# A graph network on one core: the last five edge steps of a layer written out in an order of their own

## What is computed

```python
msg = jax.nn.relu(h[src] + edge_attr) + EPS_MSG
m = msg * t
seg_max = jax.ops.segment_max(m, dst, num_segments=N)
ex = jnp.exp(m - seg_max[dst])
denom = jax.ops.segment_sum(ex, dst, num_segments=N)
agg = jax.ops.segment_sum(msg * (ex / denom[dst]), dst, num_segments=N)
z = jax.nn.relu(_layernorm((h + agg) @ w1 + b1, g1, bb1))
return z @ w2 + b2
```

## Time and profile before

| what | value |
|---|---|
| median of three runs | 8966.54 us |
| the profiled execution: its time | 8967.96 us |
| the profiled execution: its span | 8966.2 us |
| VectorE busy | 6407.4 us, 71% |
| GpSimd busy | 6370.8 us, 71% |
| ScalarE busy | 3236.4 us, 36% |
| TensorE busy | 1074.9 us, 12% |
| DMA | 1288 MB, 144 GB/s on average |

### The profile page before, as it was taken

The page is one execution under the profiler, slowest core; times in us unless marked ns, Lnnn a source line. Parts: engine busy times, 40 slices in busy tenths (PEclk is TensorE's granted clock), DMA queues, the critical chain, the costliest instruction groups (busy, mean ns, idle before and its releaser), DMA issues.

```text
span 8966.2 us, 43989 instructions
## 1 busy us (share of the span) xinstructions
PE 1074.9 (12%) x3019; PEld 778.9 (9%) x3019; DVE 6407.4 (71%) x10611; ACT 3236.4 (36%) x7064; POOL 6370.8 (71%) x6739
## 2 busy tenths in 40 slices
PE   4333333332100000000210000000020000000003
PEld 3222222221100000000100000000020000000002
DVE  7777777776577777777657777777756777777775
ACT  3444444443333333333333333333333333333332
POOL 6777777776477777777557777777746777777773
PEclk6555565555555555555555555555555555555555
DMA  6666666663244444444234444444423444444442
GB/s 193 202 200 206 205 203 201 204 204 123 70 142 138 136 136 139 140 137 136 92 89 136 136 139 141 137 136 136 141 74 102 138 141 138 136 136 141 139 137 66
DMA packets 439687, 1288.07 MB, mean 144 GB/s; under 512 B 159659, under 2 KB 173652, under 8 KB 361812
## 3 DMA queue, kind: packets, MB, share of 16 engines
q1 hardware_dynamic: 221668, 1049.13, 32.2%
q0 software_dynamic: 217968, 238.47, 13.1%
HBM read 575.00 MB, written 712.10 MB: 144 GB/s over the span
## 4 chain that ended last, share of the span: by engine, by line
DVE 24%; POOL 19%; DMA 14%; issue 10%; ACT 6%; PE 3%; DVEq 0%; POOLq 0%; ACTq 0%; SPq 0%
POOL gathered L501 18%; DMA gathered<-node_table,idx_s 13%; DVE rows_out L1070 5%; DVE run L1060 3%; DVE track L1030 3%; DVE run L1056 3%; DVE psum L1018 3%; DVE psum L1048 3%; DVE psum L1043 3%; ACT track L700 2%; ACT psum L707 1%; PE psum L610 1%; PE psum L627 1%; DVE psum L1158 1%; ACT psum L721 1%
## 5 line engine op out<-in xcount | busy, mean ns | idle before, releaser
L501 POOL DMA_INDIRECT gathered<-node_table,idx_s x6464 | 6102.9, 944 | 2243.0 <-issue 1892.7
L714 ACT ACTIVATE decay<-psum 128x512 f32<-128x512 f32 x808 | 482.6, 597 | 4935.6 <-DVE psum L1043 4935.6
L1010 DVE STREAM_TRANSPOSE psum<-gathered 128x512 f32<-128x512 f32 x808 | 576.8, 714 | 2140.6 <-DMA gathered<-node_table,idx_s 2140.3
L1030 DVE TENSOR_TENSOR_SCAN track<-psum,track,edges 128x256 f32<-128x256 f32 x1616 | 1110.1, 728 | 0.0
L1056 DVE TENSOR_TENSOR_SCAN run<-decay,run,psum 128x256 f32<-128x256 f32 x1616 | 1102.1, 721 | 0.0
L1060 DVE TENSOR_TENSOR_SCAN run<-decay,run,psum 128x256 f32<-128x256 f32 x1616 | 1097.0, 720 | 0.0
L1070 DVE STREAM_TRANSPOSE rows_out<-run 128x1024 f32<-128x1024 f32 x808 | 971.3, 1202 | 0.6
L543 PE MATMUL psum<-attr_s,edgew_s 128*128 128x256 f32 x1616 | 746.0, 641 | 1242.2 <-ACT made_s L646 1225.5
L700 ACT ACTIVATE track<-psum,bias_col 128x256 f32<-128x256 f32 x1616 | 679.6, 471 | 213.5 <-DVE psum L1018 163.4
L588 PE MATMUL psum<-cst,tails 128*3 128x128 f32 x48 | 10.9, 414 | 6208.9 <-DVE tails L1109 6128.2
L543 PEld LDWEIGHTS psum<-attr_s,edgew_s 128*128 128x128 f32 x1616 | 500.8, 325 | 1485.9 <-ACT made_s L646 1355.4
(11 more groups left out here) (167 smaller groups left out, 1513.2 us busy)
## 6 DMA issues: line engine op xcount, KB each, us to landing
edge_state<-rows_out SPq DMA_DIRECT2D x404, 1024.0 KB, 10.8
edges<-edge_rows SPq DMA_DIRECT2D x406, 640.0 KB
tracks<-track SPq DMA_DIRECT2D x404, 513.0 KB
gathered<-node_table,idx_s POOLq DMA_INDIRECT x6464, 2.8
edge_rows<-made_s SPq DMA_DIRECT2D x101, 640.0 KB, 9.6
attr_s<-in_attr SPq DMA_DIRECT2D x101, 512.0 KB, 10.5
made_s<-resets SPq DMA_DIRECT2D x101, 128.0 KB
node_table<-tab SPq DMA_DIRECT2D x27, 224.0 KB, 2.4
```

The lines of the kernel that those rows point to most:

```text
L501: pool.indirect_dma_start(gathered[u][:, at:at + C], None, table, bass.IndirectOffsetOnAxis(ap=idx_s[u][:, col:col + 1], axis=0)).then_inc ...
L1010: v.transpose(turned[s].rearrange("p (q b e) -> p b q e", q=2, e=LANES), gathered[u][:, W * st:W * st + W]).then_inc(turn_done, 1)
L1030: last = v.tensor_tensor_scan(maxima[u][:, at:at + N], logit[s][:, N * q:N * q + N], reset_s[u][:, N * st:N * st + N], carried[:, RUN * q ...
```

## The change

VectorE's loop now ends one quad earlier, chunk 196 is written out as a usual step, and the last five chunks' operations (z = 197 to z+4 = 201) stand in an order of their own, `catch_up`. The operations are the same, each once. In this order the sums are brought up step by step from three chunks behind to one chunk behind (`sums(z + 2)`, which is chunk 199, now stands ahead of `turn(z + 4)`), and what is behind the last turn is the add, the sums and the leave of 200, and the maximum, the differences, the sums and the leave of 201. On ScalarE only the step of the last chunk changes: clip and exponents of 199 and 200 come ahead of the messages of 201. In the diff, `peak` is `run_maxima`, `differ` is `differences`, `leave` is `turn_sums`, and `sums` is a wait for the previous chunk's sums, `weigh` and `run_sums`.

```diff
--- before.py
+++ after.py
@@ -723,12 +723,23 @@
                 def chunk(n, k, j, i, last):
                     s, u = i % 2, i // 2
                     begun = not isinstance(k, int) or k >= 2
-                    if begun:
+                    if last:
                         clip(n - 2, i)
-                    messages(n, j, i)
-                    if begun:
                         exponents(n - 2, i)
-                    logits(n, i)
+                        clip(n - 1, i - 1)
+                        exponents(n - 1, i - 1)
+                        messages(n, j, i)
+                        logits(n, i)
+                        clip(n, i)
+                        exponents(n, i)
+                    elif begun:
+                        clip(n - 2, i)
+                    if not last:
+                        messages(n, j, i)
+                        if begun:
+                            exponents(n - 2, i)
+                        logits(n, i)
                     if s == 1:
                         following = 2 * j + u + 2
                         copy_idx(u if isinstance(j, int) and following >= PAIRS else following, u)
@@ -737,10 +748,6 @@
                             act.wait_ge(product_out[1 - u], 16 * (j + 1 + u))
                         act.wait_ge(product_done, n + 2 * LEAD + 1)
                         copy_products(1 - u, s)
-                    if last:
-                        for n, i in ((n - 1, i - 1), (n, i)):
-                            clip(n, i)
-                            exponents(n, i)
 
                 chunk_quads(act, layer, chunk, tail=6)
 
@@ -1087,23 +1094,89 @@
                     add_products(n, j, i)
                     if at >= 3:
                         run_sums(n - 3, back(3)[1], at == 3)
-                    if last:
-                        run_maxima(n - 1, *back(1))
-                        turn_sums(n - 3, *back(3))
-                        differences(n - 1, back(1)[1], False)
-                        weigh(n - 2, back(2)[1])
-                        run_sums(n - 2, back(2)[1], False)
-                        run_maxima(n, j, i)
-                        turn_sums(n - 2, *back(2))
-                        differences(n, i, True)
-                        weigh(n - 1, back(1)[1])
-                        run_sums(n - 1, back(1)[1], False)
-                        turn_sums(n - 1, *back(1))
-                        weigh(n, i)
-                        run_sums(n, i, False)
-                        turn_sums(n, j, i)
-
-                chunk_quads(v, layer, chunk)
+                def catch_up():
+                    def place(k):
+                        return layer * CHUNKS + k, k // 4, k % 4
+                    def turn(k):
+                        turn_edges(*place(k))
+                    def add(k):
+                        add_products(*place(k))
+                    def peak(k):
+                        run_maxima(*place(k))
+                    def differ(k):
+                        differences(layer * CHUNKS + k, k % 4, k == CHUNKS - 1)
+                    def sums(k):
+                        n = layer * CHUNKS + k
+                        v.wait_ge(accumulated, n)
+                        weigh(n, k % 4)
+                        run_sums(n, k % 4, False)
+                    def leave(k):
+                        turn_sums(*place(k))
+                    z = CHUNKS - 5
+                    peak(z - 2)
+                    turn(z)
+                    leave(z - 4)
+                    differ(z - 2)
+                    sums(z - 3)
+                    add(z)
+                    sums(z - 2)
+                    peak(z - 1)
+                    turn(z + 1)
+                    leave(z - 3)
+                    differ(z - 1)
+                    add(z + 1)
+                    peak(z)
+                    differ(z)
+                    sums(z - 1)
+                    turn(z + 2)
+                    leave(z - 2)
+                    leave(z - 1)
+                    add(z + 2)
+                    peak(z + 1)
+                    differ(z + 1)
+                    sums(z)
+                    turn(z + 3)
+                    leave(z)
+                    add(z + 3)
+                    peak(z + 2)
+                    differ(z + 2)
+                    sums(z + 1)
+                    leave(z + 1)
+                    peak(z + 3)
+                    differ(z + 3)
+                    sums(z + 2)
+                    leave(z + 2)
+                    turn(z + 4)
+                    add(z + 4)
+                    sums(z + 3)
+                    peak(z + 4)
+                    leave(z + 3)
+                    differ(z + 4)
+                    sums(z + 4)
+                    leave(z + 4)
+                for i in range(4):
+                    chunk(layer * CHUNKS + i, i, 0, i, False)
+                with v.Fori(1, (CHUNKS - 6) // 4) as j:
+                    for i in range(4):
+                        chunk(layer * CHUNKS + 4 * j + i, 4 * j + i, j, i, False)
+                k = CHUNKS - 6
+                chunk(layer * CHUNKS + k, k, k // 4, k % 4, False)
+                catch_up()
 
                 sums_end = run[1][:, :].rearrange("p (x w) -> p x w", w=N)[:, :, N - 1]
                 v.tensor_copy(tails[:, 2:6], sums_end).then_inc(tail_ready, 1)
```

## The result

The changed kernel takes 8951.88 us, the kernel before 8965.59 us in the same comparison (medians of 20 runs each): ratio 0.9985, 95% interval 0.9978 to 0.9991. The forecast was 8955.5 in a range of 8947 to 8965, with 11.2 us gained.

A forecast was written before the change was run, and what follows sets the result against it. GpSimd's gathers set the pace, but at a layer's end VectorE's 27 us of remaining work does. Gains of 3.7 us in the first layer and 2.5 in three others, 11.2 us, gave 8955.5 us, range 8947 to 8965.

The forecast's parts named there:

- Waits that go, waits that come: VectorE at a layer's end: 10.4 us of waits go, 6.8 come, so the last leave ends 3.6 to 3.8 earlier.
- (a): New wait of the sums of 195 for their exponents, which stand behind the messages of 197 on ScalarE: 2.1 us.
- (b): New wait of the sums of 196 behind the add of 198, with a maximum and differences between: 0.5 us.
- (e): New wait of the sums of 201 for clip and exponents of 201, with nothing left to put between: 2.5 us.
- (d): Eight VectorE operations now directly follow what they depend on: 8 times 0.21 is 1.7 us.
- Turns 199, 200 and 201: Possible waits of these turns for gathers' landings: taken as 0, at their bad ends 0.7, 2.3 and 0.7 us.
- the tail of a few engines: Before even chunks' turns, a few DMA engines still work on stores and gathers stand in line: about 5 us idle.
- From VectorE to GpSimd: Track and the bias add hold the head gathers; row gathers start 2.5 us earlier a layer, 3.7 in the first.
- Sum: Gain over the four layers: 3.7 + 3 times 2.5 = 11.2 us.
- nothing under 18 us could be told from no change: Whole-kernel measurement: about 0.2%, 18 us, is what it can tell from no change.
- the idle time turns into gain in full: Rival: all 10.4 us of VectorE's idle time is gained, 8.5 us a layer, 8932 in all; chance 0.14.
- The slower rival: At the turn of 201 the last gathers stand behind the moved stores: 5.5 us a layer, 8989; chance 0.05.

The follow-up runs named there:

- tracks16_before: The kernel before, with track stored as one block of 64 rows instead of four of 16: 8964.58 us against 8964.91, ratio 0.9999.
- bias_in_wait_2: The changed kernel with the bias add between the differences and the sums of 201: 8944.61 us against 8964.91 for the kernel before, ratio 0.9978.
- exponents_first_2: The changed kernel with ScalarE's exponents of 195 and 196 ahead of the messages of 197 and 198: 8963.47 us, kernel before 8980.94, ratio 0.9981.
- transfers_doubled: The changed kernel with 2.3 MB of unneeded loads beside each layer's last gathers: 8968.74 us, kernel before 8980.94, ratio 0.9987.

## Why the prediction was right, step by step

- *Waits that go, waits that come.* 4.91 and 5.03 went, as said. Of those that came, (a) was put at 2.1 and is 1.98, (b) 0.5 and is 0.37, (e) 2.5 and is 2.37. The last leave ends 4.0 us earlier (mean of the layers) instead of 3.6 to 3.8. (d), eight times 0.21 or 1.7 us, was too large: in the fourth layer's timeline the eight operations start 0.11 to 0.21 us late, 1.1 in all (the leave at 8754.40 is the one with 0.21: 1.49 from the start of the scans instead of 1.28). That the sum still came out is partly luck: delays that I had at nothing, such as 0.19 ahead of the turn of 198, make 0.5 us, and of the twice 0.21 that were to go the second is 0.12.
- *Turns 199, 200 and 201.* I took nothing for each, and none waits. The turn of 200 is the one where this could have failed by 2.3 us. The reason I gave was half right: the pair's transfers start earlier (fourth layer: pair 98's 19.3 us before the last gather starts instead of 16.4, pair 99's 2.6 before it instead of 3.5 behind it) and the gathers land in time, but the wait of 5 us isn't owed to the tail of a few engines, as tracks16_before shows. That the turn of 200 costs nothing is in part luck: by the record of semaphores its rows land 0.28, 0.43, 0.03 and 0.02 us before it starts in the four layers, so in two of them VectorE and the rows arrive together. The turn of 201 had a margin of 1.5 to 2.0.

```profile
8733.52 0.34 SPq L389 DMA_DIRECT2D edges<-edge_rows  x1
...
8750.26 0.34 SPq L389 DMA_DIRECT2D edges<-edge_rows  x1
```

- *From VectorE to GpSimd.* `track` was to be there 25.5 us after the last gather and is at 25.2; the first head gather was to start inside the bias add and end at 0.77 behind it: it starts at 8777.95, the add ends at 8780.13, the gather at 8780.92, so 0.79. The row gathers gain 3.8 in the first layer (said: 3.7) and 2.7 to 3.0 in the others (said: 2.5). `track` comes 2.0 earlier where I had 1.7. bias_in_wait_2 turned this step from an argument into a measurement.
- *Sum.* 12.2 us at the layers' ends against 11.2 said. The term that was too small is the last leave's shift, by 0.3 us a layer. The other 1.5 of the 13.7 us were in no term. That nothing under 18 us could be told from no change was too cautious: the interval of the ratio leaves out 1.
- *Rivals.* That the idle time turns into gain in full is refuted by exponents_first_2: take away the avoidable waits and VectorE waits for gathers. The slower rival's mechanism is there, a delay of nearly 5 us for the last gathers, but it ends 1.5 to 2.0 us short of costing anything, and transfers_doubled didn't lengthen it.

## What to carry to other kernels

When an engine with idle time behind a pacing engine works off its backlog before the end, the end comes earlier by the waits that go less the waits that come, not by the work that is moved: here 12 us of work were moved ahead of the last turn, 10 us of waits went, some 6 came, and 4 us stayed. Then follow the gain into the next engine: a quarter of it was lost there (3.0 us a layer arrived), to an addition that could have run elsewhere, and moving that addition brought another 7.5 us for two lines. And ask of each wait where it would go: a wait that a pace imposes moves when its cause is taken away.

## What the runs showed of the hardware that I had not expected

Loads of 2.3 MB more, issued beside the last gathers, did not delay the turn that waits for them (9.2 us with and without), nor the gathers' last packets (5.9 us after the last gather starts, without them 6.8). A 128x3136 addition on VectorE held an indirect gather on GpSimd, which otherwise takes 0.9 us, until 0.77 to 0.79 us after its end whenever the gather started while the addition ran (35 cases in nine traces). And one program took 8965 to 8981 us in four comparisons and 10486 us in one on another chip, with waits of up to 3.7 us ahead of an operation whose inputs its own engine had made.
